# A graph network's count matrix with the node itself in it: the last of 64 edge places holds the node, and its one is taken off the third sum's diagonal

## What is computed

```python
agg = jax.ops.segment_sum(x[src], dst, num_segments=N)      # _gin_conv, used twice in layer 0
h = x + agg
h = jax.nn.relu(h @ Wa + ba)
return h @ Wb + bb
...
y = _mlp3(node_features[source], WM1, bM1, WM2, bM2, WM3, bM3)   # layer 1
z = jax.ops.segment_sum(y, destination, num_segments=node_features.shape[0])
return _mlp3(jnp.concatenate([node_features, z], axis=-1), WU1, bU1, WU2, bU2, WU3, bU3)
```

## Time and profile before

| | |
|---|---|
| runs, us | 962.27, 962.47, 972.05; median 962.47 |
| the profiled execution | 967.23 us, its span 965.4 us, mean granted PE clock 0.977 |
| busy share of the span | PE 92%, DVE 72%, ACT 50%, POOL 41% |
| the build | from 0 to about 410 us |
| the first pass, with layer 0's first network ahead of it | from about 412 to 770 us |
| the second pass | from 770.5 us to the end |

### The profile page before, as it was taken

The page is one execution under the profiler, slowest core; times in us unless marked ns, Lnnn a source line. Parts: engine busy times, 40 slices in busy tenths (PEclk is TensorE's granted clock), DMA queues, the critical chain, the costliest instruction groups (busy, mean ns, idle before and its releaser), DMA issues.

```text
span 965.4 us, 25212 instructions
## 1 busy us (share of the span) xinstructions
PE 883.4 (92%) x11282; PEld 717.6 (74%) x11282; DVE 699.6 (72%) x656; ACT 479.8 (50%) x573; POOL 396.0 (41%) x281
## 2 busy tenths in 40 slices
PE   0556999899899999989999999999999989999996
PEld 0235988788899999958777777777777866777774
DVE  7773999899799999576445566555555577677773
ACT  2634545556445554264455445445555454555551
POOL 5874398888300000030665546660010143444450
PEclk9967999999999999999999999999999999999998
DMA  3020544244244444333434443344432367788871
GB/s 108 19 84 17 158 124 150 84 151 143 85 136 137 137 136 136 104 115 96 132 117 121 127 125 108 112 134 116 128 106 85 103 196 216 218 240 242 239 222 49
DMA packets 81857, 126.86 MB, mean 131 GB/s; under 512 B 10288, under 2 KB 58544, under 8 KB 81616
## 3 DMA queue, kind: packets, MB, share of 16 engines
q1 hardware_dynamic: 78608, 121.98, 41.8%
q0 software_dynamic: 3136, 3.22, 1.4%
HBM read 84.22 MB, written 40.94 MB: 130 GB/s over the span
## 4 chain that ended last, share of the span: by engine, by line
PE 51%; DVE 4%; ACT 1%; issue 0%; POOL 0%; DVEq 0%; POOLq 0%; ACTq 0%
PE net_ps_hi L1270 14%; PE net_ps_lo L1270 14%; PE net_ps_hi L1287 14%; PE net_ps_mt L1213 4%; PE net_ps_ft L1213 2%; PE net_ps_check L1305 1%; DVE net_wide L832 1%; DVE hT L925 1%; DVE hT L920 1%; ACT net_wide L1109 1%; DVE net_first L932 1%; PE net_ps_mt L1317 0%; POOL net_wide L878 0%; PE net_ps_mt L1357 0%; PE net_ps_hi L1213 0%
## 5 line engine op out<-in xcount | busy, mean ns | idle before, releaser
L1270 PE MATMUL net_ps_hi<-net_wide,net_first 128*128 128x512 f32 (+1 forms) x637 | 248.5, 394 | 1.3 <-POOL net_wide L878 1.3
L1270 PE MATMUL net_ps_lo<-net_wide,net_first 128*128 128x512 f32 (+1 forms) x637 | 240.8, 382 | 0.0
L338 DVE TENSOR_TENSOR build_hot_lo<-build_grid_lo,build_keys_t 128x4096 bf16<-128x4096 bf16 x100 | 225.7, 2284 | 19.3 <-remote 16.3
L832 DVE CAST net_wide<-net_raw 128x3584 fp32r<-128x3584 uint8 (+1 forms) x90 | 203.6, 2270 | 43.7 <-PE net_ps_hi L1287 28.9
L589 PE MATMUL build_ps_out<-build_parts_pad,build_cnts 128*128 128x195 bf16 x2401 | 231.3, 253 | 2.9 <-issue 1.5
L1109 ACT ACTIVATE net_wide<-net_raw 128x3584 fp32r<-128x3584 uint8 (+1 forms) x64 | 193.6, 3025 | 78.3 <-PE net_ps_lo L1270 44.9
L456 ACT ACTIVATE build_cnts<-build_ps_cnt 128x980 uint16<-128x980 f32 (+3 forms) x176 | 150.9, 901 | 152.0 <-PE build_ps_cnt L569 117.4
L589 PEld LDWEIGHTS build_ps_out<-build_parts_pad,build_cnts 128*128 128x128 fp8e4 x2401 | 209.4, 99 | 8.7 <-issue 3.8
L1287 PE MATMUL net_ps_hi<-net_wide,net_second 128*128 128x512 f32 (+1 forms) x637 | 157.7, 397 | 3.6 <-ACT net_wide L1109 2.0
L1287 PEld LDWEIGHTS net_ps_hi<-net_wide,net_second 128*128 128x128 f32 x637 | 113.6, 188 | 43.5 <-issue 13.7
L1270 PEld LDWEIGHTS net_ps_hi<-net_wide,net_first 128*128 128x128 f32 x637 | 119.8, 188 | 31.9 <-issue 7.0
(11 more groups left out here) (167 smaller groups left out, 688.5 us busy)
## 6 DMA issues: line engine op xcount, KB each, us to landing
net_raw<-edge_counts SPq DMA_DIRECT2D x168, 448.0 KB, 3.8
edge_counts<-build_cnts SPq DMA_DIRECT2D x168, 224.0 KB
xres<-in_x SPq DMA_DIRECT2D x1, 1568.0 KB, 7.1
net_raw<-edge_counts SPq DMA_DIRECT2D x14, 112.0 KB, 2.0
out<-xres SPq DMA_DIRECT2D x12, 128.0 KB, 4.0
build_rows<-in_dst_rows,build_row_i POOLq DMA_INDIRECT x49
build_edges<-in_edges,build_start_i POOLq DMA_INDIRECT x49, 4.3
edge_counts<-build_cnts SPq DMA_DIRECT2D x7, 112.0 KB
```

What stands on the lines that cost most here:

```text
L338: return v.tensor_tensor(hot.rearrange("p c (k t) -> p c k t", t=2), grid[:, :].rearrange("p (k t) -> p k t", t=2)[:, None, :, :].broadcas ...
L832: return issue(expanded[e % WIDE_RING][:, 0:n, :, :].rearrange("p w a d -> p (w a d)"), raw[e % RAW_RING][:, 0:n, :, :].rearrange("p w a d ...
L1270: last = nc.tensor.matmul(ps[(b + 1) % 2][:, 0:n * P], first[:, c, lo:lo + H], expanded[e % WIDE_RING][:, 0:n, k, :], start=(c == 0), stop ...
```

## The change

A run's last place no longer holds an edge: the constant HELD = 63 is new, the keys of place 63 are written once by POOL (source row = the node's own row, window = its own window), and `find_keys` works on places 0 to 62. So each count's diagonal already has the node's own one in it. The first sum leaves out the product by `small_b`, and `use` runs over 49 products a window in place of 50. In the first pass `add_own` and its waits are gone. In the second pass the third sum must not have the node itself, so POOL subtracts the identity from the owned tiles: `take_own(e)` waits for the cast of piece e, subtracts, and `use2` waits for it (`own_taken`) at the 18 owned pieces. It stands in POOL's program order behind POOL's own cast of the same piece, or between the casts of the pieces before and after. Ahead of the second pass POOL has the casts of pieces 0 and 1 and then the seven tallies, each behind a block of the first pass. The check compares with E + NW * P, since each node now has one key more.

```diff
+HELD = RUN - 1
...
-        small_b = sb("small_b", [P, P], BF16)
...
+                nc.gpsimd.iota(keys[:, 0, 0:NW, HELD], [[0, NW]], 0, 1, **kw).then_inc(consts, 1)
+                nc.gpsimd.iota(keys[:, 1, 0:NW, HELD], [[1, NW]], 0, 0, **kw).then_inc(consts, 1)
...
-                    v.tensor_scalar(small_b[:, :], ramp[:, :], part[:, 0:1], SMALLEST, ALU.is_equal, ALU.mult)
...
-                    link(v.tensor_scalar(tile_no[:, 0:n, :], src, 7, None, ALU.logical_shift_right))
+                    link(v.tensor_scalar(tile_no[:, 0:n, 0:HELD], src, 7, None, ALU.logical_shift_right))
...
-                        if c < NW:
-                            last = nc.tensor.matmul(to, cnts[u % A_RING][:, w % 2, c, :],
-                                                    parts66[:, c, :, with_check], start=(c == 0), stop=False)
-                        else:
-                            last = nc.tensor.matmul(to, small_b[:, :], parts66[:, w, :, with_check],
-                                                    start=False, stop=True)
+                        last = nc.tensor.matmul(to, cnts[u % A_RING][:, w % 2, c, :], parts66[:, c, :, with_check],
+                                                start=(c == 0), stop=(c == NW - 1))
...
-                def add_own(b):
-
-                    for e in pieces(0)[b * PIECES:(b + 1) * PIECES]:
-                        if e not in own_pieces:
-                            continue
-                        engine, count = EXPAND[e]
-                        pool.wait_ge(grown[engine], count)
-                        for j, k in own_tiles(e):
-                            tile = expanded[e % WIDE_RING][:, j, k, :]
-                            last = nc.gpsimd.tensor_tensor(tile, tile, ident[:, :], ALU.add)
-                        last.then_inc(own_added, 1)
+                def take_own(e):
+
+                    engine, count = EXPAND[e]
+                    pool.wait_ge(grown[engine], count)
+                    for j, k in own_tiles(e):
+                        tile = expanded[e % WIDE_RING][:, j, k, :]
+                        last = nc.gpsimd.tensor_tensor(tile, tile, ident[:, :], ALU.subtract)
+                    last.then_inc(own_taken, 1)
...
                 for e in pieces(1):
                     if EXPAND[e][0] == "pool":
                         expand(pool, nc.gpsimd.tensor_copy, e).then_inc(grown["pool"], 1)
+                    if e in own_pieces:
+                        take_own(e)
...
                 def use2(e):
                     b, i = ORDER[e]
                     engine, count = EXPAND[e]
-                    pe.wait_ge(grown[engine], count)
+                    if e in own_pieces:
+                        pe.wait_ge(own_taken, own_pieces.index(e) + 1)
+                    else:
+                        pe.wait_ge(grown[engine], count)
```

60 lines of the change are left out of this document (25 added, 35 removed).

## The result

The changed kernel takes 995.08 us (median of 4 runs, 984.29 to 1008.09), the kernel before 967.26 us beside it (median of 4, 962.27 to 977.75): a ratio of 1.0238, 95% interval 1.0153 to 1.0323. A second comparison gave 986.49 against 959.03 us, 1.0343 (1.0261 to 1.0424). So the change makes the kernel slower by some 2.4 to 3.4%; the forecast was 992 us, or 1.031 times the median of 962.47. The profiled run of the changed kernel took 989.71 us, its span 987.9.

The account below looks back on a forecast made before the run. The prediction took PE and DVE as full in the build and PE as the bound in both passes. 34.5 - 3.9 - 1.3 = +29.3 us gave 996.5 for the profiled run, 992 us at the median; range 975 to 1003.

Parts of the forecast that it names:

- The removed products: Build: leaving out 49 small products on PE saves 3.9 us, between nothing and 4.5.
- The 1.6 us at the end of the build: Build's end: PE nearer to DVE's last one-hots gains 1.3 us with the handoff, three small products behind 0.3.
- The other 2.3 us: Build up to 263.81 us: small products of 25 windows, 92 ns each, come through as 2.3 us saved.
- The wait in the first pass: First pass: PE's idle time put down to POOL's diagonal additions goes away, saving 1.3 us, bounds 0 and 2.
- The stalls with the port held: Second pass: PE waits for POOL's tiles, delayed by DVE casts holding the shared port; 34.5 us added, chance 0.55.
- the follow-up waits of POOL's casts: Second pass, blocks 2 and 7: POOL's next cast queues behind its tiles and holds PE 1.6 us more.
- The clock: Rival, second pass: PE's clock falls after six stalls of 2.7 us or more, adding 10 us: 1002 us; chance 0.18.
- The base: Whole kernel: the sum was put on the profiled run of 967.23 us, then shifted to the median of 962.47.
- Not slower: Rival, second pass: tiles are hidden, 957 us; within 1% if stalls stay under 15 us; chance 0.07.
- The tiles don't lose the port: Rival, second pass: stalls are latency alone, 18.5 us, so +13.3 in all, 976 us; chance 0.17.

Follow-up runs that it names:

- e3: The changed kernel without POOL's 49 subtractions and PE's wait for them, node itself left in the third sum: ratio 0.9799 to the kernel before.
- e7: The changed kernel without the subtraction, with 49 products by a matrix of zeros put back in the build: ratio 0.9886 to the kernel before.
- after: The changed kernel as first profiled, set against the kernel before: profiled run 989.71 us, ratio 1.0238.
- e10: The changed kernel with each DVE cast of the second pass in four instructions instead of one: ratio 1.0097 to the kernel before.
- e4: The changed kernel with POOL's subtractions at the same places but on other memory, PE waiting for casts alone: ratio 1.0234 to the kernel before.
- e8: The changed kernel without POOL tiles: ACT keeps each node's own message, DVE's copy of the third sum subtracts it; ratio 0.9935 to the kernel before.
- e11: The changed kernel with the 49 tiles subtracted by DVE instead of POOL, which only casts: ratio 0.9869 to the kernel before.
- before: The kernel without the change, as first profiled: profiled run 967.23 us, build 410.6 us.

## Why the forecast was right, and where not

- **Direction and total: right, the total by luck.** 49 tiles between cast and PE make the second pass slower, and e3 shows that nothing else does. The total holds two errors that nearly cancel (the clock and the base, below).
- **The removed products, -3.9 us: right in the part that the traces can show.** The 1.6 us at the end of the build came out as 1.3 to 1.75. The other 2.3 us fit the 4.0 us between e3 and e7, but that is within the spread of one and the same build.
- **The wait in the first pass, -1.3 us: right.** 331.0 to 329.2 us, 1.8 us less, wherever PE waits for no tile at the second pass's start. In after itself the start of block 0 takes it back: PE waits 1.69 us there (1.8 forecast).
- **The stalls with the port held, 34.5 us: the mechanism right, a little large.** PE's idle time rose by 28.7 us in the second pass and 1.7 at its start; its waits for POOL come to 31.8. Block by block, with the forecast in brackets, they are 2.3 (1.8), 0 (0.4), 3.8 (5.2), 2.7 (4.2), 2.5 (2.7), 1.3 (1.4), 1.1 (1.1), 3.5 (4.6), 5.4 (6.7), 4.5 (3.0), 3.6 (2.2) and 1.1 (1.2) for blocks 0 to 11. In block 3 the tiles of p1 met no DVE cast, and the follow-up waits of POOL's casts were shorter than 1.6 us (1.24 in block 2, 0.58 in block 7). e10 is the direct test of "whichever has begun finishes": shorter casts, shorter waits. The rule of the Trainium skill that I set beside it ("Advanced Engine Details and Errata", section "VectorE Performance Modes": the shared port makes the two engines block each other) agrees with e10's 656 ns a tile against 867. That a waiting DVE cast goes ahead of POOL's next tile came out too, but not for the reason given, POOL's own semaphore: in block 2 a DVE cast of 2.16 us begins during the first of four tiles, and the second, ahead of which POOL waits for nothing, takes 2.24 us.
- **The clock: this step failed.** I set it beside the sum as a rival at 0.18, on the ground that PE is full between the stalls, and a fall of the clock in the second pass was one of the signs that I named for being wrong. The sum left out 16.8 us: in six places the clock is at the lower level at or behind a pause. The rival's 10 us were too few as well: it had six spells of 4 us at 0.57, and there were 37.5 us at 0.50. Both courses, port and clock, came together. The Trainium skill, "TensorE: Matmul & The Clock Gate", Part 1, has idleness throttle the array. The windows of after agree (0.50 from 882 to 887 us, behind 2.54 busy us of 5), and I weighed it too lightly; which pause brings a fall differs between the two traces of the changed kernel.
- **The base: this step failed too.** I laid the sum on a profiled run whose build held a pair of 29.8 us, where the same pair took 12.7 in after, and took the build for steady. By the stages, the second pass cost 45.5 us and the first 0.2; less some 4 for the products that is about 42 us, against 29.3 forecast. The build of after was shorter by another 19 us that the sum has no term for, and that leaves the 22.5 us between the spans. The missing clock term and the missing shorter build nearly cancel, and so it is luck that the total fell where it was forecast. The medians agree: they differ by 27.8 and 27.5 us in the two comparisons, far less than the second pass's 42 to 46.
- *Not slower* fell: PE's idle time is twice the 15 us that it allowed. *The tiles don't lose the port* (18.5 us) fell as well, by e10 and by the 28.7 us.

## What to carry to other kernels

An instruction put between a cast and its reader costs more than its own time: here 49 tiles of 0.43 us, 21 us in all, became 45 (after against e3), and two thirds of that stayed when nobody waited for the tiles (e4), because the engine's next cast stood behind them. Where a sum has to be corrected on the diagonal, correct the result, which is small, and not the operand (e8). And before a difference of a few per cent is put down to an edit, cut both traces into stages, and set the stages against the medians of many runs: here a stage that the edit hardly touched moved by 23 us.

## What the runs showed that was not expected

- Pauses of PE of 1.7 to 4.5 us in an otherwise full pass stood ahead of 3.4 to 10.2 us at a granted clock of 0.50, in six places, and that cost 16.8 us besides 28.7 us of idle time. Others of 2.5 and 2.6 us did not. In e11, whose pauses within the pass are of 1.65 us at the most, the clock fell only where the pass begins, behind 3.5 us.
- In all five traces with a long first pair in the build the clock was still at the lower level when that pair began; in all nine without, it had risen by then.
- PE's counting products stood still for 0.5 to 1.2 us at a time with nothing that the trace shows to wait for, 18.7 us in the build of before and 9.1 in that of after; in before half of it lay beside gathers of under 1 us. With the gathers spaced it was 4.7 us, in a build in which PE also waited longer for others.
- POOL's gathers took 0.94 us where DVE stood still, and mostly 1.9 to 3.1 us where it was busy. From 40 to 250 us in before, ten of the 17 gathers under 1 us met no DVE instruction, and all 54 of 1.89 us and more had DVE busy for over half of their time.
